# Four-layer graph network in fp32: the order of work at the passage into the last layer, the place of its row sums, and the order of its last group

## The reference

```python
# layer 2: attention with 8 heads of 64 inside each graph; mask = adj + adj
q, k, v = proj(Wq, bq), proj(Wk, bk), proj(Wv, bv)
attn = softmax(q @ k.T * SCALE * mask, axis=-1)
x = x + (attn @ v) @ Wo.T + bo
# layer 3: three matmuls with hops over a row-normalised transition matrix
Xw = h @ Wv + bv;  sj = Xw @ aw[:d];  si = Xw @ aw[d:]
alpha = A * exp(leaky_relu(sj[None, :] + si[:, None] + ab, 0.2))
T = alpha / (sum(alpha, axis=-1) + 1e-12)
H = (h @ Wk[0] + bk[0]) + (T @ h @ Wk[1] + bk[1]) + (T @ T @ h @ Wk[2] + bk[2])
x = x + relu(H)
```

## Time and profile before

| | us |
|---|---|
| median of 3 runs | 2275.75 |
| profiled execution, its own time | 2281.91 |
| span of its trace | 2280.1 |
| TensorE busy in it | 2246.0 |
| VectorE / ScalarE / GpSimd busy | 1314.0 / 784.9 / 717.8 |
| mean granted TensorE clock | 0.995 |

### The profile page before, as it was taken

The page is one execution under the profiler, slowest core; times in us unless marked ns, Lnnn a source line. Parts: engine busy times, 40 slices in busy tenths (PEclk is TensorE's granted clock), DMA queues, the critical chain, the costliest instruction groups (busy, mean ns, idle before and its releaser), DMA issues.

```text
span 2280.1 us, 39533 instructions
## 1 busy us (share of the span) xinstructions
PE 2246.0 (99%) x15903; PEld 1779.9 (78%) x15903; DVE 1314.0 (58%) x2645; ACT 784.9 (34%) x1401; POOL 717.8 (31%) x926
## 2 busy tenths in 40 slices
PE   8999999999999999999999999999899999999998
PEld 5778888888888877888888888888677777777776
DVE  3565565565655665554656455665665757575752
ACT  3332332333322333233333333232343434343432
POOL 2343343334333423223332223332351313131320
PEclk9999999999999999999999999999899999999999
DMA  6223333333333343332333332333444343535341
GB/s 199 75 75 96 96 107 102 84 92 94 84 95 96 102 135 111 99 101 80 85 101 92 101 97 80 91 105 93 123 123 111 84 114 82 129 68 127 71 106 37
DMA packets 185048, 224.75 MB, mean 99 GB/s; under 512 B 68688, under 2 KB 85152, under 8 KB 184864
## 3 DMA queue, kind: packets, MB, share of 16 engines
q1 hardware_dynamic: 179104, 214.35, 35.1%
q10 hardware_dynamic: 5760, 7.87, 1.4%
HBM read 88.91 MB, written 50.37 MB: 61 GB/s over the span
## 4 chain that ended last, share of the span: by engine, by line
PE 90%; SPq 3%; DVE 3%; DMA 2%; ACT 1%; issue 1%; POOL 1%; DVEq 0%; ACTq 0%
PE bank L329 49%; PE bank L319 28%; PE bank L345 3%; PE bank L603 3%; SPq L1430 2%; PE bank L533 1%; PE bank L503 1%; PE bank L309 1%; PE bank L380 1%; DMA si<-stB 1%; PE bank L296 0%; DVE hs L668 0%; DMA arows<-stB 0%; DMA small<-in_L_gnn_ab 0%; ACT g1T L1037 0%
## 5 line engine op out<-in xcount | busy, mean ns | idle before, releaser
L329 PE MATMUL bank<-w_hi,h3T_hi 128*128 128x512 f32 x768 | 306.4, 399 | 1.8 <-ACT Z L988 1.8
L329 PE MATMUL bank<-w_lo,h3T_hi 128*128 128x512 f32 x768 | 300.3, 391 | 0.0
L329 PE MATMUL bank<-w_hi,h3T_lo 128*128 128x512 f32 x768 | 300.0, 391 | 0.0
L1235 POOL TENSOR_SCALAR stA<-stA 128x4 f32<-128x4 f32 x48 | 11.5, 239 | 682.8 <-DVE stA L645 682.7
L1002 ACT ACTIVATE hn<-x,stA 128x512 f32<-128x512 f32 x192 | 140.7, 804 | 233.9 <-POOL stA L1240 228.0
L643 DVE BATCH_NORM_STATS2 stA<-x 128x6 f32<-128x512 f32 x192 | 128.3, 668 | 149.2 <-DMA x<-mid 148.8
L329 PEld LDWEIGHTS bank<-w_hi,h3T_hi 128*128 128x128 f32 x768 | 144.7, 188 | 56.8 <-issue 25.2
L988 ACT ACTIVATE Z<-bank 64x512 f32<-64x512 f32 x256 | 151.7, 593 | 96.1 <-PE bank L329 78.8
L329 PEld LDWEIGHTS bank<-w_hi,h3T_lo 128*128 128x128 f32 x768 | 144.8, 188 | 30.6
L329 PEld LDWEIGHTS bank<-w_lo,h3T_hi 128*128 128x128 f32 x768 | 144.8, 189 | 29.0
L1248 POOL TENSOR_TENSOR h1T_lo<-hGB,h1T_hi 128x512 fp32r<-128x512 f32 x64 | 80.6, 1288 | 200.9 <-ACT h1T_hi L988 200.9
(11 more groups left out here) (217 smaller groups left out, 5720.8 us busy)
## 6 DMA issues: line engine op xcount, KB each, us to landing
hGA<-hs SPq DMA_DIRECT2D x768, 64.0 KB, 2.0
mid<-x SPq DMA_DIRECT2D x32, 1024.0 KB, 4.5
x<-mid SPq DMA_DIRECT2D x32, 1024.0 KB, 6.2
x<-in_x SPq DMA_DIRECT2D x16, 1024.0 KB, 5.9
hGB<-hs SPq DMA_DIRECT2D x256, 64.0 KB, 2.0
out<-x SPq DMA_DIRECT2D x15, 1024.0 KB, 9.5
blk<-in_adj SPq DMA_DIRECT2D x128, 64.0 KB
PT<-hs SPq DMA_DIRECT2D x120, 64.0 KB, 2.1
```

Of the source, the lines that this page charges most:

```text
L329: ins = eng.matmul(b[:], h[l][:, k, ts], W[r][:, k, :], start=(k == 0 and i == 0), stop=(last and k == 3 and i == 2))
```

## The change

- Layer 2, last group: VectorE runs the whole softmax and the additions VV before the eight sums of layer 3's group 0, which had been done in two parts around the softmax. ScalarE runs both halves of the exponentials before it splits W3[2] and W3[1], and copies PT before it makes the high features of layer 3's group 0. GpSimd splits W3[2] before it makes the low features.
- Layer 3: the row sums of group g are asked by TensorE after two z2 products of group g itself (in group 0 after two z1 products). VectorE takes them after `stats_A(3, g+2)` and `l3_alpha(g+1)`, ahead of `transposes(3, g+2)`; in group 0 before `adj_T(3, 1)`. GpSimd makes Town(g) after `scale_A(3, g+2)` and before `l3_alpha(g+1)`; ScalarE makes Tother(g) after `norm_A(3, g+2)`.
- SyncE issues `load3(2)` straight after `gather(3, 1)`.
- Last group: y and its hop run for tiles 0 and 2 first, then for tiles 1 and 3.

```diff
--- before.py
+++ after.py
@@ -588,14 +588,14 @@
-            def l3_hop(zi, name, g):
+            def l3_hop(zi, name, g, rs=(0, 1)):
...
                 pe.wait_ge(a_zh[zi], 8 * g + 8)
-                for r in range(2):
+                for r in rs:
                     for p, c in ((0, 0), (1, 1), (0, 1), (1, 0)):
@@ -604,24 +604,33 @@
+            def l3_y(g, t):
+                gemm_open(("y", g, t), hT3[g % 2], t, W3[0], (v_y, 4 * g + (1, 3, 2, 4)[t]), False)
+
             for g in range(NG):
...
                     gemm(("z2", g, t), hT3[i], t, W3[2], (a_zh[0], 8 * g + 2 * t + 2))
-                    if g == 0 and t == 1:
-                        l3_rowsum(0)
+                    if g and t == 1:
+                        l3_rowsum(g)
                 pe.wait_ge(p_wlo, lo_pool["w1"])
...
                     gemm_open(("z1", g, t), hT3[i], t, W3[1], (a_zh[1], 8 * g + 2 * t + 2), False)
+                    if g == 0 and t == 1:
+                        l3_rowsum(0)
                 l3_hop(0, "z1", g)
                 pe.wait_ge(p_wlo, lo_pool["w0"])
-                for t in range(4):
-                    gemm_open(("y", g, t), hT3[i], t, W3[0], (v_y, 4 * g + (1, 3, 2, 4)[t]), False)
-                    if t == 1 + (g == 0) and g + 1 < NG:
-                        l3_rowsum(g + 1)
-                l3_hop(1, "y", g)
+                if g + 1 < NG:
+                    for t in range(4):
+                        l3_y(g, t)
+                    l3_hop(1, "y", g)
+                else:
+                    for r in range(2):
+                        l3_y(g, r)
+                        l3_y(g, 2 + r)
+                        l3_hop(1, "y", g, (r,))
@@ -893,8 +902,6 @@
                     l2_ctx(g - 1, 1)
-                if g == NG - 1:
-                    l3_sums(dve, eng, 0, (0, 1))
                 for u in range(2):
@@ -909,8 +916,6 @@
                     dve.wait_ge(d_bv2, 16)
-                    if g == NG - 1:
-                        l3_sums(dve, eng, 0, (2, 3))
                     for t in range(4):
@@ -920,6 +925,8 @@
                         eng.tensor_tensor(VV[:, t, :], bank.of(("v2", g, t))[:], bv2, ALU.add).then_inc(v_vv, 1)
+                    if g == NG - 1:
+                        l3_sums(dve, eng, 0, range(4))
@@ -932,18 +939,19 @@
                 if g == 0:
-                    l3_rowsum(0)
                     l3_sums(dve, eng, 1, (2, 3))
...
                     stats_A(3, g + 2)
+                if g == 0:
+                    l3_rowsum(0)
                 if g + 1 < NG:
...
                     l3_alpha(g + 1)
+                if g:
+                    l3_rowsum(g)
                 if g + 2 < NG:
...
                     l3_sums(dve, eng, g + 2, range(4))
-                if g + 1 < NG:
-                    l3_rowsum(g + 1)
                 xt = xs[x_slot(kA(3, g))]
@@ -956,16 +964,14 @@
             dve.wait_ge(d_sc, 16 * (g - 1))
-            first = g == 0 and 0 in ts
             if g == 0:
                 dve.wait_ge(v_cst, 1)
-                if not first:
-                    dve.wait_ge(*bank.done(("qk", NG - 1, 3)))
+                dve.wait_ge(*bank.done(("qk", NG - 1, 3)))
             for t in ts:
...
                 for c in range(2):
-                    dve.wait_ge(v_dotA, 8 * g + 2 * t + c - (not first))
-                    unused = sc3[:] if first else yt[c][:] if g < 2 else junk[:, c, :]
+                    dve.wait_ge(v_dotA, 8 * g + 2 * t + c - 1)
+                    unused = yt[c][:] if g < 2 else junk[:, c, :]
                     eng.scalar_tensor_tensor(unused, hn[t][:], 0.0, arow[:, c, :], ALU.max, ALU.mult,
@@ -1156,17 +1162,14 @@
                     l2_exp(g, 0)
+                    l2_exp(g, 1)
                     if g == NG - 1:
...
                         split_in_place(W3[1], d_w1)
-                    l2_exp(g, 1)
                 if on:
...
                     features2_hi(2, g + 1, hT2[(g + 1) % 2])
-                elif on:
-                    act.wait_ge(v_dotA, 4)
-                    features2_hi(3, 0, hT3[0])
                 if g == 0:
@@ -1185,6 +1188,8 @@
                              bank.of(("pT", r))[:].rearrange("p (c q n) -> p c q n", c=4, q=4)).then_inc(a_pt, 1)
+                    act.wait_ge(v_cst, 1)
+                    features2_hi(3, 0, hT3[0])
@@ -1207,18 +1212,18 @@
                     l3_z(0, ("z2", g, t), g, t)
-                    if g == 0 and t == 1:
-                        l3_T_other(0)
+                if g == 0:
+                    l3_T_other(0)
                 if g + 2 < NG:
                     norm_A(3, g + 2)
+                if g:
+                    l3_T_other(g)
                 if g + 1 < NG:
...
                     l3_z(1, ("z1", g, t), g, t)
-                if g + 1 < NG:
-                    l3_T_other(g + 1)
@@ -1326,8 +1331,8 @@
                     pool.wait_ge(p_bones, 3)
+                    split_in_place(W3[2], "w2")
                     features_lo(3, 0, hT3[0], hGA, p_flo3)
-                    split_in_place(W3[2], "w2")
                     scale_A(3, 1)
@@ -1564,6 +1570,7 @@
                     gather(3, 1)
+                    load3(2)
                 if g == NG - 1:
@@ -1581,7 +1588,6 @@
             eng.dma_start(bkb[:], L3_gnn_bk.partition_broadcast(128)).then_inc(d_bk3, 16)
-            load3(2)
             for g in range(NG):
...
                 if g == 0:
```

## The result

The changed kernel takes 2305.76 us, the median of 4 runs (2302.63 to 2308.46), against 2275.98 (2275.45 to 2278.11) for the kernel before: ratio 1.0127, 95% interval 1.0115 to 1.0139. It is 29.8 us slower. The forecast was 2298.5, range 2281 to 2312. The profiled execution of after took 2308.46 with a span of 2306.7, which is 26.6 more than before's span; the sum of the prediction said 22.8.

The account below looks back on a forecast made before the run. TensorE, busy 2246.0 of 2280.1 us, was taken as the bound, with a hidden layer 3 reload loop equally slow. Terms -1.0 + 17.8 + 7.8 - 1.8 = +22.8 us, from the median 2275.75, gave 2298.5 us, range 2281 to 2312.

Parts of the forecast that it names:

- The passage (part 1): End of layer 2: context starts 9.2 us earlier, but TensorE then waits some 7 us for cT_lo; one or two left.
- Group 0 (part 2): Start of layer 3: first y product about 2.6 us late, reload of group 1 1.0 us earlier than before.
- The hop behind the reload (3a): Layer 3: each hop waits for its round's reload, 9.9 us after landing instead of 2.1, so 7.8 us later.
- The loop (3b): Layer 3, groups 1 to 13: the row sum lengthens the reload loop by 17.8 us over twelve rounds.
- 12 x 2.12 = 25.4: Layer 3 loop: the row sum's VectorE time over twelve rounds, before subtracting 5.2 and 2.4 us; also the upper bound.
- the 13.9 us of its upper bound: End of layer 2: all eight sums ahead of cT_lo slow, 8 x 1.74 us, putting cT_lo at 1654.0.
- The pairs (4): Last group: fewer VectorE operations follow the last hop, 1.8 us less, bounds 0 to 2.7.
- Reload of group 1: Start of layer 3: it lands 1.0 us earlier than before, entering the sum as -1.0 us.
- Cold hops: Rival, layer 3: waits at the hops slow TensorE's clock, 8 us more than forecast, 2307 us; chance 0.13.
- The faster case: Rival, layer 3: the row sum stays hidden, hops stay 37.3 us apart, 2266 us; chance 0.09.

Follow-up runs that it names:

- the passage alone: The kernel before with only the new order at the end of layer 2 and load3(2) moved: 2278.08 us, ratio 0.9999.
- The added VectorE operations: Two useless VectorE operations ahead of transposes(3, g+2): in the kernel before 2283.65 us, ratio 1.0027; in the changed kernel 2307.99 us, ratio 1.0127.
- the pairs alone: The kernel before with only the last group's y and hop in two pairs: 2277.51 us, ratio 0.9995.

## Why the prediction was right, and where it wasn't

**The passage (part 1).** Right to 0.5 us: context at 1642.05 (1641.6 said), cT_lo at 1652.63 (1652.4), the wait 6.96 (some 7). Six sums were slow, by the eight durations of L975 from 1640.98. That nothing of it that can be measured reaches the end is shown by the passage alone.

**Group 0 (part 2).** W3[0] is late by 2.3 us (2.6 said); the reload of x that the earlier trace rows show landed 5.7 us earlier, at 1683.35 (3 to 6 said). The reload of group 1 landed 0.2 us earlier than before and not 1.0. The half clock after the wait of 7.0 us (0.50 in 1650 to 1660) isn't the cause: before has such a stretch too, 0.68 and 0.81 in 1640 to 1660, and from 1663 us to the landing no wait of VectorE ended with TensorE. The timelines show where the time went. VectorE had sirows 2.4 us earlier, at 1698.24 against 1700.59 in the earlier trace rows. But GpSimd scaled the statistics of the reloaded x only behind Town(0), the split of W3[0] and the sums of the biases, so the norm on ScalarE came late, and the exponential stands behind it. The norm and the exponential, first in after, then in before:

```profile
1699.29 2.94 ACT L1008 ACTIVATE hn<-x,stA 128x512 f32<-128x512 f32 x4 [9.05 <-POOL stA L1245]
1702.13 0.40 ACT L1142 ACTIVATE ec<-ec 128x256 f32<-128x256 f32 x1
...
1694.55 2.93 ACT L1002 ACTIVATE hn<-x,stA 128x512 f32<-128x512 f32 x4 [13.15 <-POOL stA L1240]
...
1701.95 0.42 ACT L1136 ACTIVATE ec<-ec 128x256 f32<-128x256 f32 x1 [4.47 <-DVE ec L863]
```

The low features therefore start where they did (1703.30, before 1703.13). The sums start 1.35 us earlier but last 1.4 us longer, with one more slow sum, and si goes out at 1712.76 against 1712.74.

**The hop behind the reload (3a).** Right: hop 13 stands 10.2 us behind its reload (2209.76 - 2199.59), 9.9 said, against 2.1 before. The 7.8 forecast is 8.0. The row sum ahead of the reload takes it away.

**The loop (3b).** The size came out right, and the delay does pass through VectorE's queue as said: the prediction charged 1.48 us a round, 17.8 in all; the sums start 1.4 us later, and from landing to si the round grew by 1.50, so 18.0. What the prediction left out is that the length of the sums depends on where they meet GpSimd. "12 x 2.12 = 25.4" prices the row sum as if the sums behind it always took the same time. The added VectorE operations show that they don't: by themselves 2 us there cost 0.3 before and 0.2 more in after, because a later start saves a slow sum, 1.1 us. In after nothing was saved, since a second thing that the sum left out took it back: Town(g) and Tother(g) stand ahead of the exponential, alt and the low features of g + 1, so these start 1.6 us later. The prediction has neither of the two terms, and they cancel. That its 17.8 came so near is in part luck.

The Trainium skill, "SBUF — State Buffer", on the shared port pair, says that a VectorE instruction with two SBUF inputs and a GpSimd instruction that reads SBUF hold the pair by an exclusive lock, so that the later one blocks fully. By it the two would take turns, one sum for each low feature; from the times of each alone, 0.6 and 1.3 us, a turn is an estimated 1.9 us. The trace agrees in kind, four low features and four slow sums, but a turn takes 1.70 us, less than the rule gives, and the measurement decides. The prediction used no term from the rule and said that by it eight sums would never cost more than the 13.9 us of its upper bound; eight turns of 1.9 us would be 15.2, so that remark doesn't hold. It should have counted the turns.

Two more things that the sum left out nearly cancel. From its issue the reload of x took 6.59 us to land and not 7.13 (mean of 12), 6.5 us less. SyncE took longer over the 16 gathers: against 10.53 us from si to the reload's issue at best, the twelve rounds have 17.6 us too much, against 10.4 before, so 7.2 more. 18.0 - 6.5 + 7.2 is 18.7, as by the landings. Such an excess stands in all traces here, 10 to 21 us in 12 rounds. And the 7.13 belong to this trace of before rather than to its kernel: in every other trace here the mean is 6.5 to 6.7. So the forecast of 22.8 can't be called good to better than several us.

**The pairs (4).** From hop 13 to the end of the last residual it is 94.4 us in before and in after (2304.1 - 2209.8). In that figure stand two things of the same size: the pairs gave 1.6 of the 1.8 said, and the wait before hop 13 took 1.6 back through the clock, with 0.66 in 2205 to 2215 and 3.5 us instead of 1.9 for the matmuls of this hop.

**The sum.** Reload of group 1: -0.2 (-1.0 said); rounds 18.7 (17.8); hop 8.0 (7.8); end 0.0 (-1.8). That is 26.5 of the 26.6 us. The medians differ by 29.8, since the profiled execution of before lay 5.9 us above its median and that of after 2.7 above its own.

**The rivals.** Cold hops: the clock did fall to 0.66 at the two longest waits, the hop behind the wait of 2.42 us ran slow too (1.12 us a row instead of 0.65), and 4.3 us of busy time were added over the span. But 9 waits and not 13 were seen, and from hop 1 to hop 13 TensorE took 39.12 us a group, the pace of the reloads, 39.13. The faster case fell with the first line of the waits. The passage alone and the pairs alone show that even without the row sums the change brings nothing that can be measured.

## What to carry to other kernels

An engine that is busy 98% of the time can hide a second loop of the same period that never touches it; find it by measuring the distance between landings of the same transfer, and put nothing behind the landing that another engine's next round waits for. When two engines slow each other instruction by instruction, time added to one ahead of the shared stretch is partly free as long as the other stays where it is; if both move, the whole delay passes through. A wait removed on the way to a queue that is already full only moves to the next tile in it: count the queue before counting the wait.

## What the runs showed of the hardware

A VectorE sum of 128x512 takes 0.68 us alone and 1.77 beside GpSimd's low features, one sum for each low feature; a low feature takes 1.29 us in the mean of layer 1 and 1.71 in that of layer 3, by the groups of the page. The issue of 16 gathers of 64 KB takes SyncE 10.0 us at best, and in some rounds of every kernel 11 to 17. In after, the waits of TensorE of 6 to 7 us came with stretches of 10 us at 0.66 and 0.50, so part or all of them ran at 1.2 GHz. Shorter waits gave both: behind 2.3, 2.9 and 3.4 us (1694.52, 1705.89, 1897.53) the granted clock stayed at 1.00, while 0.83 was granted in 2088 to 2098 around the wait of 2.42 us, and before had 0.75 around its waits of 1.9 and 1.8 us.
